# An expert stage that fetches its token rows by number inside its loop, with biases added by VectorE

## The chip, the cores and the metric

One Trainium2 chip, one of its cores. The time is that of one execution of the whole program on the device, in microseconds (us). The engines of a core are TensorE (PE), VectorE (DVE), ScalarE (ACT), GpSimd (POOL) and SyncE (SP); each runs its own list of instructions, and they wait for each other by semaphores. SP here only issues transfers; POOL issues those whose rows are chosen by a table of numbers in SBUF (indirect transfers).

## What is computed

A decoder layer on x of shape (8, 256, 256), so 2048 tokens of width D = 256: a gated linear branch, cross attention, self attention, and at its end a mixture of 8 experts, which is what the change is about:

```python
gp = softmax(xt @ w_group + b_group)          # 4 groups of 2 experts
g_idx, g_prob = argmax(gp), max(gp)
ep_sel = softmax(elog)[g_idx];  e_idx_local, e_prob = argmax(ep_sel), max(ep_sel)
flat_e = g_idx * 2 + e_idx_local              # one expert of 8 for each token
combine = one_hot(flat_e, E) * (g_prob * e_prob)
h = relu(einsum('td,edf->etf', xt, w1) + b1)  # 256 -> 512
y = einsum('etf,efd->etd', h, w2) + b2        # 512 -> 256
out = einsum('te,etd->td', combine, y)
x = layernorm(x + out)                        # of norm(x) with gain and bias
```

## The kernel before

`build` runs three stages with a barrier between them. `gate_stage` (in the profile 0 to 86 us) computes the weights of the linear branch from x @ qkv in a loop over pairs of batch rows; SP loads the next x of the pair as soon as TensorE has transposed the one before. Beside it GpSimd fills the DRAM table `xs_d` with zeros and a dummy token number (`blank`, L290 to L293, 5.9 MB). `attention_stage` (86 to 770 us) does both attentions, and writes for each batch row two results to DRAM: `x5_d` (the experts' input) and `x4_d` (the value to be added at the end). `w1`, the experts' first weights, is loaded at its start; it also makes an fp32r copy of a small table `chunk` (L1276).

`moe_stage` (770 us to the end) has two parts. The first sorts the tokens by expert: VectorE works out each token's expert, gate and rank (L1670 to L1742) with two small matrix products for the counts (L1586, L1587), and a row number `slot` in a table of 23 tiles of 128 rows (`TILES = NT + E - 1`, each tile of one expert, padded). SP loads all 2048 rows of `x5_d` and `x4_d` into `xr` (L1525, L1527); GpSimd writes them with 16 indirect transfers (L1558) to their places in `xs_d`, gate and token number among them as columns `GATE` and `TOKEN`. Then the second part runs over the 23 tiles. For tile c:

- SP loads the tile's 128 rows of `xs_d` into one of six buffers `xs` (L1536), once `u` of the tile six before is made.
- TensorE transposes it (L1599), multiplies with `w1` of the tile's expert (L1607), transposes the hidden rows (L1624) and multiplies with `w2` (L1616). The expert's number is read into a register from `texp_i` (`expert`, L1515) twice for each tile. Ahead of each of the two products a short fp32r product (L1605, L1614) puts the expert's bias into PSUM: `sel`, a 0/1 matrix, picks it from `bs`, which holds high and low parts of the biases.
- ScalarE moves the transposes from PSUM (L1642, L1652) and does the ReLU (L1647).
- VectorE: `first_b` to `first_e` (L1763 to L1777) scale by the gate, add the row itself and take mean and variance; `second_a` to `second_d` (L1784 to L1797) and `shift` (L1801) do the last normalisation. The parts of tile c and of tile c-1 are interleaved, so that hardly an instruction stands right behind the one it depends on.
- GpSimd takes two inverse roots for each tile (L1565, L1569) and writes the tile's output rows to their tokens (L1575, indirect).

TensorE's list is skewed by hand: the transposes of tile c+2, then the first product of tile c+1, then the second product of tile c-1, then the transposes of the hidden rows of tile c. `done(engine, semaphore, c)` is a wait for tile c.

Of the kernel before, what the change touches and what calls it, by code (L numbers as in the profile page):

```python
# [23 lines left out]
P = 128  # L24
# [15 lines left out]
ROW = 2 * D + 2  # L40
# [11 lines left out]
def build(nc, I, out):  # L52
# [8 lines left out]
    x4_d = scratch("x4_d", (B, P, T * D))  # L61
    x5_d = scratch("x5_d", (B, P, T * D))
    xs_d = scratch("xs_d", (TILES * P, ROW))

    outer = ExitStack()
    with outer:
# [18 lines left out]
        w1 = sbo("w1", [P, E, C, F])  # L85
        dense = outer.enter_context(ExitStack())

        def sbd(name, shape, dt=F32):
# [8 lines left out]
                 "bfeat": sbd("bfeat", [2 * C, 3, P]), "chunk": sbd("chunk", [2 * C, C * S]),  # L97
# [9 lines left out]
        def next_stage():  # L107
# [5 lines left out]
        gate_stage(nc, I, sem, ident, nhalf, stat, xsum, chan, wtok, dw, ahead, pT, pD, pS, vT_d, xs_d)  # L113
        next_stage()
        attention_stage(nc, I, sem, ident, nhalf, chan, wtok, logit, dw, w1, ahead, pT, pD, pW,
                        vT_d, x4_d, x5_d)
        next_stage()
        dense.close()
        moe_stage(nc, I, sem, ident, nhalf, logit, w1, bank, x4_d, x5_d, xs_d, out)
# [45 lines left out]
def gate_stage(nc, I, sem, ident, nhalf, stat, xsum, chan, wtok, dw, ahead, pT, pD, pS, vT_d, xs_d):  # L165
    with ExitStack() as ctx:
# [15 lines left out]
        blank = sb("blank", [P, ROW])  # L182
# [19 lines left out]
        def sems(names):  # L202
            return (sem("g_" + n) for n in names.split())

        w_in, small_in, w_hi, w_lo, mask0, masks, zero_ok, zero_out = sems(
            "w_in small_in w_hi w_lo mask0 masks zero_ok zero_out")
        dw_in, ahead_in = sems("dw_in ahead_in")
# [17 lines left out]
        def _(sp):  # L225
# [30 lines left out]
            sp.dma_start(ahead["chunk"][:, :], I["chunk"]).then_inc(ahead_in, 16)  # L256
# [3 lines left out]
            sp.wait_ge(ahead_in, 16 * 11)  # L260
# [5 lines left out]
        def _(pool):  # L266
# [19 lines left out]
            for m in (selb, selq):  # L286
# [3 lines left out]
            pool.memset(blank[:, 0:2 * D + 1], 0.0).then_inc(zero_ok, 1)  # L290
            pool.memset(blank[:, 2 * D + 1:ROW].bitcast(I32), B * S).then_inc(zero_ok, 1)
            pool.wait_ge(zero_ok, 2)
# [5 lines left out]
            pool.wait_ge(zero_out, 16)  # L298
# [124 lines left out]
        def _(dve):  # L423
# [128 lines left out]
            step(dve.tensor_copy(wtok[:, :, :].rearrange("p t b -> p (t b)"), pS[1][:, 0:T * B]))  # L552

# [66 lines left out]
def attention_stage(nc, I, sem, ident, nhalf, chan, wtok, logit, dw, w1, ahead, pT, pD, pW,  # L620
                    vT_d, x4_d, x5_d):
    with ExitStack() as ctx:
# [290 lines left out]
        def _(pe):  # L913
# [65 lines left out]
            def attention(i, l, a, beside):  # L979
                if i == 0 and a == 0 and l == 0:  # L980
                    pe.wait_ge(bias_ok, 5)
# [463 lines left out]
def moe_stage(nc, I, sem, ident, nhalf, logit, w1, bank, x4_d, x5_d, xs_d, out):  # L1445
    with ExitStack() as ctx:
# [97 lines left out]
        def _(pool):  # L1544
# [17 lines left out]
            for c in range(TILES + 4):  # L1562
# [8 lines left out]
                if there(c - 3):  # L1571
                    if c == 3:
                        pool.wait_ge(ids_in, 16)
# [313 lines left out]
```

## Time and profile before

| | us |
|---|---|
| median of 3 runs | 956.08 |
| lowest and highest | 943.71, 959.67 |
| the profiled execution | 957.81 |
| its span, from the first to the last instruction | 955.9 |
| mean granted TensorE clock in it (share of full) | 0.832 |

| stage | us in the profiled execution |
|---|---|
| gate stage | 0 to 86 |
| attention stage | 86 to 770 |
| expert stage, sorting | 770 to 815.2 |
| expert stage, 23 tiles | 815.2 to 955.9 |

Rows of the profile read: start, duration, engine, line, operation, output <- input, and in square brackets how long the engine had been idle before, and who ended that. A busy time of TensorE is modelled at its end, so the distance from start to start tells more than the duration. The biggest of these times, the attention stage, is touched by the change only at its edges.

### The profile page before, as it was taken

To read this page: it belongs to the slowest core of one execution; us is meant where nothing else is said; L and a number is where in the kernel's file an instruction comes from. 1 tells how busy PE (TensorE), PEld (TensorE's weight loads), DVE (VectorE), ACT (ScalarE), POOL (GpSimd) and SP (SyncE) were. 2 spreads that over 40 slices of the span, in tenths; PEclk is the share of its full clock that TensorE was granted. 3 is DMA by queue.
4 is the path that set the end of the run, shared out by engine and by line. 5 is a ranking of instruction groups with operands and counts; after the bars stand their busy time and mean duration, and the time that the engine had idled before them with its cause. 6 is when DMAs were issued, how large, how long until landed. Compare 5 with 4: busy or idle time off the path is not lost. (4 is left out here: it accounts for less than half of the span.)

```text
span 955.9 us, 11735 instructions
## 1 busy us (share of the span) xinstructions
PE 722.9 (76%) x4012; PEld 453.6 (47%) x4012; DVE 469.8 (49%) x1248; ACT 261.5 (27%) x397; POOL 182.4 (19%) x211
## 2 busy tenths in 40 slices
PE   4852487879887797878878888878896810899993
PEld 3741354545544454545545455544554410456562
DVE  1885165564653626455354745637456252044443
ACT  1101032323324221342404224232240300233432
POOL 1003410112201111220101122011110016034445
PEclk9985779988898867988779797987987655799997
DMA  9582612223112130311123031220303069222210
GB/s 281 147 278 70 195 35 67 50 64 78 46 34 68 46 80 32 78 46 34 51 62 84 30 78 46 57 56 2 78 2 89 3 219 328 67 61 69 77 59 14
DMA packets 66015, 77.88 MB, mean 81 GB/s; under 512 B 10758, under 2 KB 53459, under 8 KB 65832
## 3 DMA queue, kind: packets, MB, share of 16 engines
q1 hardware_dynamic: 60792, 62.56, 24.0%
q0 software_dynamic: 3872, 12.37, 4.1%
q10 hardware_dynamic: 1296, 2.23, 0.7%
q8 instruction: 33, 0.54, 0.2%
q14 instruction: 22, 0.18, 0.1%
HBM read 32.76 MB, written 19.57 MB: 55 GB/s over the span
## 5 line engine op out<-in xcount | busy, mean ns | idle before, releaser
L1337 DVE TENSOR_REDUCE a_nmax<-wide 128x4 f32<-128x1024 f32 x128 | 153.2, 1217 | 72.8 <-PE wide L975 72.3
L1187 ACT ACTIVATE a_E<-wide 128x1024 f32<-128x1024 f32 x128 | 123.5, 1013 | 50.6 <-PE wide L975 50.5
L857 POOL TENSOR_TENSOR a_rstd<-a_var,nhalf 128x2 f32<-128x2 f32 x40 | 27.9, 698 | 546.6 <-DVE a_var L1302 546.6
L133 PE MATMUL bank<-a_th,dw 128*128 128x256 f32 x320 | 108.0, 484 | 6.4 <-DVE a_x L1312 5.0
L975 PE MATMUL wide<-a_Q,a_K 50*128 50x256 f32 x512 | 73.3, 377 | 33.2 <-DMA a_Q<-a_mrow 18.6
L964 PE MATMUL bank<-a_E,a_va 128*32 128x256 f32 x1024 | 91.5, 490 | 0.0
L133 PE MATMUL bank<-dw,a_th 128*128 128x256 f32 x320 | 88.9, 412 | 0.0
L133 PEld LDWEIGHTS bank<-a_th,dw 128*128 128x128 f32 x320 | 70.5, 237 | 33.2 <-issue 14.3
L975 PE MATMUL wide<-a_K,a_Q 48*128 48x256 f32 x512 | 70.9, 363 | 20.3 <-DMA a_Q<-a_stage 13.0
L1166 ACT ACTIVATE a_th<-bank 128x512 f32<-128x512 f32 x48 | 28.6, 597 | 201.6 <-PE bank L922 201.6
L975 PEld LDWEIGHTS wide<-a_Q,a_K 50*128 50x128 f32 x512 | 46.0, 225 | 74.6 <-ACT a_E L1187 33.9
L133 PEld LDWEIGHTS bank<-dw,a_th 128*128 128x128 f32 x320 | 62.5, 205 | 28.6 <-ACT a_th L1166 10.0
L975 PEld LDWEIGHTS wide<-a_K,a_Q 48*128 48x128 f32 x512 | 43.9, 212 | 62.8 <-issue 37.5
L1763 DVE SCALAR_TENSOR_TENSOR m_z<-wide,m_xs 128x256 f32<-128x256 f32 x23 | 11.1, 484 | 96.9 <-PE wide L133 96.9
L1288 DVE TENSOR_TENSOR a_stage<-bank,a_stage 128x256 fp32r<-128x256 f32 x64 | 24.1, 419 | 65.2 <-ACT a_stage L1174 65.2
L1359 DVE COPY a_cu<-bank 128x256 f32<-128x256 f32 x64 | 25.7, 419 | 49.3 <-PE bank L964 49.3
L133 PE MATMUL bank<-w,m_xT 128*128 x92 | 49.2, 660 | 0.0
L964 PEld LDWEIGHTS bank<-a_E,a_va 128*32 128x32 f32 x1024 | 31.9, 129 | 32.3 <-issue 22.2
L133 PE MATMUL wide<-m_w,m_hT 128*128 x184 | 45.9, 392 | 0.9 <-ACT m_hT L1652 0.9
L1174 ACT ACTIVATE a_stage<-bank 128x512 fp32r<-128x512 f32 x32 | 19.1, 597 | 74.4 <-PE bank L133 67.2
L133 PEld LDWEIGHTS wide<-m_w,m_hT 128*128 128x128 f32 x184 | 33.1, 189 | 7.5 <-issue 1.3
L1198 ACT ACTIVATE a_mrow<-bank 8x256 fp32r<-8x256 f32 x32 | 12.0, 374 | 89.3 <-PE bank L1026 88.7
(256 smaller groups left out, 985.0 us busy)
## 6 DMA issues: line engine op xcount, KB each, us to landing
a_K<-a_stage SPq DMA_DIRECT2D x96, 128.0 KB, 3.2
a_Q<-a_stage SPq DMA_DIRECT2D x96, 128.0 KB, 3.5
xs_d<-g_blank POOLq DMA_DIRECT2D x1, 5911.0 KB, 28.2
m_xs<-xs_d SPq DMA_DIRECT2D x23, 257.0 KB, 2.7
w<-in_w_dram SPq DMA_DIRECT2D x1, 4096.0 KB
x_d<-a_x SPq DMA_DIRECT2D x16, 256.0 KB, 2.7
m_xr<-x_d SPq DMA_DIRECT2D x16, 256.0 KB, 5.5
m_w<-in_w_dram SPq DMA_DIRECT2D x1, 4096.0 KB, 24.8
```

Source lines behind the costliest of these rows:

```text
L133: last = pe.matmul(out, left[c], right[c], start=(start and c == 0), stop=(stop and c == n - 1))
L857: pool.tensor_tensor(rstd[l][:, :], var[l][:, :], nhalf[:, 0:T], ALU.pow).then_inc(rs_ok[l].s, 1)
L964: last = pe.matmul(bank[32 * h:32 * h + 32, 0:S], va[l][:, kt, HC * (h // 2) + 2 * g + h % 2, :], Ex[g % 2][:, kt, h, :], start=(kt == 0), ...
L975: last = pe.matmul(pW[r % 2][:, c * 512 + e * S:c * 512 + (e + 1) * S], left[l][part_, s, tok(t)], right[l][part_, s, :], start=True, stop ...
L1166: act.activation(halves(dst[l]), pT[l][:, :], ACT.Copy).then_inc(done[l].s, 1)
L1174: act.activation(stage[l][:, x_, :, 0, :], bank[l][:, :].rearrange("p (c s) -> p c s", c=C), ACT.Copy).then_inc(done[l].s, 1)
L1187: act.activation(Ex[g % 2][:, kt, :, :], pW[r % 2][:, :].rearrange("p (h s) -> p h s", h=4), ACT.Exp, scale=HD ** -0.5).then_inc(ex.s, 1)
L1198: act.activation(mrow[:, h, 0, :], pT[l][0:HC, h * S:(h + 1) * S], ACT.Copy).then_inc(mx_hi[l].s, 1)
L1288: last = dve.tensor_tensor(stage[l][:, x_, c, 1, :], bank[l][:, c * S:(c + 1) * S], stage[l][:, x_, c, 0, :].bitcast(F32), SU)
L1337: dve.tensor_reduce(nmax[l][:, t, :].rearrange("p (h c q e) -> p h q c e", h=HALVES, c=C, q=2)[:, jj // 2, jj % 2, :, :], pW[r % 2][:, :]. ...
L1359: dve.tensor_copy(cu[:, g, :], (pT, pD)[g % 2][l][:, 0:S]).then_inc(cu_ok[l].s, 1)
L1763: dve.scalar_tensor_tensor(z[c % 2][:, :], pY[c % 2][:, 0:D], xs[c % XB][:, GATE:GATE + 1], xs[c % XB][:, 0:D], MM, AD).then_inc(z_ok, 1)
```

## The change

- `xs_d`, `x4_d`, `x5_d` and `xr` are gone, with the fill in the gate stage. The attention stage writes both results side by side into one table `xc_d` of 2048 rows of 512 columns, in token order (pieces of 1 KB instead of 2 KB).
- The numbers of the tokens of each tile are made by 16 matrix products: `place` (a 0/1 matrix for each block of 128 tokens: which row in its tile) times `want` (for each token: its tile, times 1, its number or its gate). The sum is `ids` (number), `gates` and, by the empty places, `oids` (output number, out of bounds where the place is empty).
- GpSimd fetches each tile's rows from `xc_d` with an indirect transfer `gather(c)`: four before the loop, and one in each turn, four tiles ahead. SP's loads are gone.
- The bias products, `sel`, `bs` and what made them are gone. `b2` is loaded spread over all partitions (1 MB) in the attention stage behind `w1`, `b1` (2 MB) at the start of the expert stage ahead of `w2`. VectorE adds them when it moves the products out of PSUM: `inner(c)` for 512 columns, `first_a(c)` for 256. VectorE reads the expert's number into a register for each. ScalarE's ReLU now sits in the move of the hidden transposes, and its move L1647 is gone.
- VectorE's list in the loop is rewritten: `inner` of the next tile, the second half of one tile, the first half of the next, with pairs that depend on each other closer together.
- TensorE waits for `w2` only before the first product that uses it. The copy of `chunk` moves to the end of the gate stage.

```diff
-            pool.dma_start(xs_d.rearrange("(p n) d -> p n d", p=P),
-                           blank[:, :].unsqueeze(1).to_broadcast([P, TILES, ROW])).then_inc(zero_out, 16)
...
+            dve.wait_ge(chunk_in, 16)
+            dve.tensor_copy(ahead["chunk_r"][:, :], chunk[:, :])
...
+            sp.dma_start(b2[:, :, :], I["b2"].partition_broadcast(P)).then_inc(w1_in, 16)
...
-            for b in range(B):
-                sp.dma_start(xr[:, b * T:(b + 1) * T, 0:D], x5_d[b].rearrange("p (t d) -> p t d", t=T)).then_inc(x5_in, 16)
...
+            sp.dma_start(b1[:, :, :], I["b1"].partition_broadcast(P)).then_inc(b_in, 16)
             sp.dma_start(w2[:, :, :, :], I["w2"].rearrange("e (c p) f -> p e c f", p=P)).then_inc(w_in, 16)
...
-            for n in range(NT):
-                pool.indirect_dma_start(out=xs_d, out_offset=bass.IndirectOffsetOnAxis(ap=slot[:, n:n + 1], axis=0),
-                                        in_=xr[:, n, :], in_offset=None).then_inc(xs_w, 16)
+            def gather(c):
+                done(pool, u_ok, c - XB)
+                pool.indirect_dma_start(out=xs[c % XB][:, :], out_offset=None, in_=xc_d,
+                                        in_offset=bass.IndirectOffsetOnAxis(ap=ids[:, c:c + 1], axis=0)
+                                        ).then_inc(xs_in[c % XB], 16)
+            pool.wait_ge(id_ok, 1)
+            for c in range(AHEAD):
+                gather(c)
             for c in range(TILES + 4):
+                if there(c + AHEAD):
+                    gather(c + AHEAD)
...
+            for n in range(NT):
+                if n % 4 == 0:
+                    pe.wait_ge(place_ok, n // 4 + 1)
+                last = pe.matmul(bank[0][:, 0:3 * TILES], place[:, n, :], want[:, n, :, :].rearrange("p k c -> p (k c)"),
+                                 start=(n == 0), stop=(n == NT - 1))
...
-                    pe.matmul(pH[l][:, :], sel[:, c + 1, :], bs[:, 0:F], start=True, stop=False)
-                    pe.matmul(pY[l][:, 0:D], sel[:, c - 1, :], bs[:, F:], start=True, stop=False)
...
-                    act.activation(hb[l][:, :], pH[l][:, :], ACT.Relu).then_inc(hb_ok, 1)
-                    act.activation(halves(hT[l]), pHT[l][:, :], ACT.Copy).then_inc(hT_ok, 1)
+                    act.activation(halves(hT[l]), pHT[l][:, :], ACT.Relu).then_inc(hT_ok, 1)
...
+            step(dve.tensor_scalar(r16[1][:, :], r16[0][:, :], 1.0 / P, None, MM))
+            step(dve.tensor_tensor(over, r16[1][:, :].unsqueeze(2).to_broadcast([P, NT, TILES]),
+                                   cst[:, NT:].unsqueeze(1).to_broadcast([P, NT, TILES]), ALU.is_ge))
+            step(dve.tensor_reduce(r16[2][:, :], over, AX.X, AD))
+            step(dve.scalar_tensor_tensor(r16[4][:, :], r16[2][:, :], -float(P), r16[0][:, :], MM, AD))
+            dve.tensor_tensor(want[:, :, 2, :], over, past[:, :, 1:], SU).then_inc(want_ok, 1)
+            for n in range(0, NT, 4):
+                dve.tensor_tensor(place[:, n:n + 4, :], line[:, :].unsqueeze(1).to_broadcast([P, 4, P]),
+                                  r16[4][:, n:n + 4].unsqueeze(2).to_broadcast([P, 4, P]), ALU.is_equal).then_inc(place_ok, 1)
...
+            dve.tensor_copy(ids[:, :], bank[0][:, 0:TILES]).then_inc(id_ok, 1)
...
+            def inner(c):
+                e = expert(dve, c)
+                done(dve, h_mm, c)
+                done(dve, h_tr, c - 2)
+                dve.tensor_tensor(hb[c % 2][:, :], pH[c % 2][:, :], b1[:, bass.ds(e, 1), :].rearrange("p o f -> p (o f)"), AD
+                                  ).then_inc(hb_ok, 1)
...
+            for c in range(-1, TILES + 3):
+                if there(c + 1):
+                    inner(c + 1)
+                if there(c - 2):
+                    second_a(c - 2)
+                    second_b(c - 2)
+                if there(c - 3):
+                    shift(c - 3)
+                if there(c - 1):
+                    first_a(c - 1)
+                if there(c - 2):
+                    second_c(c - 2)
+                if there(c - 1):
+                    first_b(c - 1)
+                if there(c - 2):
+                    second_d(c - 2)
+                if there(c - 1):
+                    first_c(c - 1)
+                    first_d(c - 1)
+                    first_e(c - 1)
```

## Rows read from the trace of the kernel before

**Rows 1.** By stretch: length; busy PE, PEld, DVE, ACT, POOL; PEclk; DMA share; GB/s.
```profile
815.20:829.00 13.80, 13.61 (x28) 5.69 (x28) 0.00 (x0) 3.00 (x7) 0.00 (x0) 0.61 0.35 78
860.00:890.00 30.00, 30.00 (x118) 18.77 (x118) 12.84 (x54) 11.64 (x23) 13.03 (x18) 1.00 0.23 72
```

**Rows 2.** Timeline: TensorE in one turn of the tile loop.
```profile
852.45 0.38 PE L1599 MATMUL bank<-ident,m_xs 128*128 128x128 f32 x2
852.76 0.49 PE L1605 MATMUL bank<-m_bs,m_sel 16*128 16x512 f32 x1
853.18 1.98 PE L133 MATMUL bank<-w,m_xT 128*128 x4
855.09 0.38 PE L1614 MATMUL wide<-m_bs,m_sel 16*128 16x256 f32 x1
855.40 1.99 PE L133 MATMUL wide<-m_w,m_hT 128*128 x8
857.23 0.60 PE L1624 MATMUL wide<-ident,m_hb 128*128 128x128 f32 x4
```

**Rows 3.** Timeline: VectorE, the first tile's product read and one turn later on.
```profile
831.40 0.48 DVE L1763 SCALAR_TENSOR_TENSOR m_z<-wide,m_xs 128x256 f32<-128x256 f32 x1 [36.80 <-PE wide L133]
...
857.43 0.48 DVE L1763 SCALAR_TENSOR_TENSOR m_z<-wide,m_xs 128x256 f32<-128x256 f32 x1 [2.90 <-PE wide L133]
```

**Rows 4.** Timeline: from the rank of each token to the first tile.
```profile
788.65 0.29 DVE L1741 TENSOR_TENSOR m_rank<-m_rank,m_oh 128x128 f32<-128x128 f32 x1
788.97 0.29 DVE L1742 TENSOR_REDUCE m_r<-m_rank 128x16 f32<-128x128 f32 x1
...
790.35 1.07 POOL L1558 DMA_INDIRECT xs_d<-m_xr,m_slot  x1 [14.16 <-DVE m_slot L1743]
...
809.47 0.96 POOL L1558 DMA_INDIRECT xs_d<-m_xr,m_slot  x1 [0.31 <-issue]
...
815.21 1.29 PE L1599 MATMUL bank<-ident,m_xs 128*128 128x128 f32 x4 [32.39 <-DMA m_xs<-xs_d]
```

**Rows 5.** Timeline: gate stage, TensorE's and VectorE's wait in its first turn.
```profile
22.45 0.66 PE L315 MATMUL wide<-ident,g_x 128*128 128x128 f32 x4 [3.85 <-DMA g_x<-in_x_dram]
...
30.10 0.69 DVE L435 TENSOR_REDUCE xsum<-wide 128x512 f32 x1 [1.00 <-ACT g_xh L393]
```

**Rows 6.** Transfers: issue, count, KB each, median us from issue to landing.
```profile
g_x<-in_x_dram SPq DMA_DIRECT2D x8, 256.0 KB, 4.1
...
xs_d<-g_blank POOLq DMA_DIRECT2D x1, 5911.0 KB, 28.2
...
out_dram<-m_o,m_ids POOLq DMA_INDIRECT x23, 2.5
```

**Rows 7.** Groups of instructions: busy us and mean ns, VectorE on 184 and 512 columns.
```profile
L1745 DVE TENSOR_TENSOR m_cmp_t<-m_cst,m_ntile 128x184 f32<-128x184 f32 x1 | 0.3, 343 | 0.0
...
L1420 DVE TENSOR_TENSOR a_va<-bank,rows 128x512 f32<-128x512 f32 x8 | 5.5, 692 | 2.9 <-PE bank L133 2.9
```

**Rows 8.** Timeline: the first of the two small products of the sorting.
```profile
781.62 0.77 PE L1586 MATMUL wide<-m_oh,m_low 128*128 128x128 f32 x2 [12.68 <-DVE m_oh L1705]
782.18 0.63 PE L1587 MATMUL wide<-m_oh,m_ones 128*128 128x128 f32 x2
```

**Rows 9.** Line L1515, TensorE's register loads: ns min/median/max, first and last start.
```profile
L1515 PEldq TENSOR_LOAD <-m_texp_i x46: 295/301/526, 815.8 to 937.2; - x46
L1515 PEldq FUSED_REGOPS  x46: 151/151/171, 816.4 to 937.6; - x46
```

**Rows 10.** Timeline: GpSimd in one turn of the tile loop.
```profile
854.17 0.73 POOL L1565 TENSOR_TENSOR m_rstd<-m_var,nhalf 128x1 f32<-128x1 f32 x1 [2.77 <-DVE m_var L1776]
...
855.60 1.03 POOL L1575 DMA_INDIRECT out_dram<-m_o,m_ids  x1 [0.19 <-issue]
```

**Rows 11.** Busy time of two output transfers' issue, columns as in Rows 1.
```profile
942.12:943.15 1.03, 0.00 (x0) 0.00 (x0) 1.03 (x4) 0.00 (x0) 1.03 (x1) 1.00 0.00 0
855.60:856.63 1.03, 1.03 (x6) 0.90 (x6) 0.00 (x0) 0.20 (x1) 1.03 (x1) 1.00 0.00 0
```

More of the change, by code:

```diff
@@ L159, in __call__, with gate_stage @@
         self.eng.wait_ge(self.sem, self.i * self.per + self.base + self.n)
-def gate_stage(nc, I, sem, ident, nhalf, stat, xsum, chan, wtok, dw, ahead, pT, pD, pS, vT_d, xs_d):
+def gate_stage(nc, I, sem, ident, nhalf, stat, xsum, chan, wtok, dw, ahead, pT, pD, pS, vT_d):
     with ExitStack() as ctx:
@@ L255, in _ @@
             sp.dma_start(ahead["bfeat"][:, :, :], I["bfeat"]).then_inc(ahead_in, 16)
-            sp.dma_start(ahead["chunk"][:, :], I["chunk"]).then_inc(ahead_in, 16)
+            sp.dma_start(chunk[:, :], I["chunk"]).then_inc(chunk_in, 16)
             sp.dma_start(ahead["part"][:, :], I["part"]).then_inc(ahead_in, 16)
@@ L627, in both @@
             return [sb(f"{name}{l}", shape, dt) for l in range(2)]
-        cin, x, pos, rows, brow, bfeat, chunk, part, wr = (
-            ahead[n] for n in "cin x pos rows brow bfeat chunk part wr".split())
-        chunk_r = sb("chunk_r", [2 * C, C * S], F32R)
+        cin, x, pos, rows, brow, bfeat, chunk_r, part, wr = (
+            ahead[n] for n in "cin x pos rows brow bfeat chunk_r part wr".split())
         bsplit = sb("bsplit", [2 * C, 3, P], F32R)
@@ L1441, with moe_stage @@
 XB, UB = 6, 4
-GATE, TOKEN = 2 * D, 2 * D + 1
-def moe_stage(nc, I, sem, ident, nhalf, logit, w1, bank, x4_d, x5_d, xs_d, out):
+AHEAD = 4
+def moe_stage(nc, I, sem, ident, nhalf, logit, w1, b2, bank, xc_d, out):
     with ExitStack() as ctx:
@@ L1453, in moe_stage @@
         w2 = sb("w2", [P, E, FC, D])
-        bias = sb("bias", [E, F + D])
-        bs, bl = sb("bs", [2 * E, F + D], F32R), sb("bl", [E, F + D], F32R)
-        which = some(3, "which", [2 * E, 1])
-        at16 = sb("at16", [2 * E, 2 * E])
-        sel = sb("sel", [2 * E, TILES, P], F32R)
-        xr = sb("xr", [P, NT, ROW])
+        b1 = sb("b1", [P, E, F])
+        past = sb("past", [P, NT, TILES + 1])
+        want = sb("want", [P, NT, 3, TILES])
+        place = sb("place", [P, NT, P])
+        line = sb("line", [P, P])
+        gate = sb("gate", [P, NT])
+        gates = sb("gates", [P, TILES])
+        free = sb("free", [P, TILES])
         gain = sb("gain", [P, D])
@@ L1629, in _ @@
             act.dma_start(gain[:, :], I["rows"][R_FG2].partition_broadcast(P)).then_inc(c_in, 16)
-            act.wait_ge(b_in, 32)
-            act.activation(bs[0:E, :], bias[:, :], ACT.Copy).then_inc(b_hi, 1)
             act.wait_ge(g_in, 1)
@@ L1802, in shift @@
                                          ).then_inc(mr_ok, 1)
-            for c in range(TILES + 2):
-                now, old, older = there(c), there(c - 1), there(c - 2)
-                if now:
-                    first_b(c)
-                if old:
-                    second_a(c - 1)
-                if now:
-                    first_c(c)
-                if old:
-                    second_b(c - 1)
-                if now:
-                    first_d(c)
-                if old:
-                    second_c(c - 1)
-                if older:
-                    shift(c - 2)
-                if now:
-                    first_e(c)
-                if old:
-                    second_d(c - 1)
+            for c in range(-1, TILES + 3):
[18 more added lines that the diff above has]
+                    first_e(c - 1)
 def layouts(inputs):
```

146 lines of the change are left out of this document (62 added, 84 removed).

## The prediction

> **What bounds the kernel now.** I read four views in this order: the stages by stretch, the timeline of the expert stage, the groups of instructions, and the first turns of the gate stage. In the 30 us between 860 and 890 us TensorE is busy for all 30, at a granted clock of 1.00 (2.4 GHz), while VectorE is busy for 12.84 and GpSimd for 13.03 [rows 1]. So the tile loop is bound by TensorE. One turn is, from start to start: input transposes 0.31, bias product 0.42, first product 1.91, bias product 0.31, second product 1.83, hidden transposes to the turn's end 0.44 [rows 2], together 5.22. VectorE's starts say the same: (857.43 - 831.40) / 5 = 5.21 [rows 3].
>
> Ahead of the loop stands a serial stretch. The tokens' ranks are done at 788.97 + 0.29 = 789.26; 16 scatters leave GpSimd from 790.35 to 809.47, one each 1.27; the last must land and be read back before the transposes at 815.21 [rows 4]. That is 25.95 us in which TensorE does nothing. In the gate stage TensorE waits 3.85 us for an x tile and VectorE 1.00 in the turn behind [rows 5], while the fill of `xs_d` takes 28.2 us to land; the median x load takes 4.1 [rows 6].
>
> **The change part by part.** The sum is made against the profiled execution, 957.81 us, which lies 1.7 above the median of 956.08.
>
> *Gate stage, -4.85 and +0.7.* Without the fill the third x load should take the usual 4.1 us. It is issued when TensorE has transposed the first tile, which is before the first products, so it is there well before TensorE's products end at 22.45 - 3.85 = 18.6. The 3.85 goes. The turn behind it waited 1.00 more on VectorE [rows 5]; from there on VectorE paces the stage, and keeps what it got. I take 4.85 (bounds 0, if the load is late for another reason, and 4.85). The copy of `chunk`, 512 columns, now stands at the end of VectorE's list: 0.69 by another 512-column operation [rows 7]. At its old place its cover was TensorE's and ScalarE's work, so nothing comes back there.
>
> *Attention stage, +0.2.* 1 MB more behind the 4 MB of `w1` is queued on SP ahead of the first key rows. In the stretches that I looked at, the DMA engines stand still for some microseconds before the query rows that the first scores wait for, so this is hidden; without that cover it costs some 3 us. Rows of 1 KB instead of 2 may let the last store land a little later: 0 to 0.5.
>
> *Sorting to first tile, -11.6.* New, behind 789.26, on VectorE: a 16-column scale 0.2; compare, reduce and difference on 16 x 23 = 368 columns. 184 columns take 0.34 and 512 take 0.69 [rows 7], so 0.54 each, and 0.03 from the end of one to the start of one that needs it [rows 4]: 3 x 0.57, with a small one of 0.22: 2.1 so far. Two more of 368 columns 0.9, the first `place` 0.69: 793.0. Then 16 products of 69 moving columns. The product of 128 columns takes 0.56 from start to start [rows 8]; if all of it goes with the columns one is 0.30, if nothing 0.56. I take 0.40, 6.4 together (bounds 4.8 and 9.0), for both matrices must be loaded, whatever moves. VectorE makes the four `place` groups in 4 x 0.69, faster than they are used. 799.4. Copy of the numbers 0.3, GpSimd's start 0.8 (its first scatter came that much behind `slot` [rows 4]), and one gather from issue to landing: not in the trace; the output writes need 2.5 [rows 6], the last scatter and its read-back together 815.21 - 809.47 = 5.7. It is nearest to the former, but of double size: 3.1. First tile there at 803.6 instead of 815.21. `b1` and `w2`, 6 MB, have 30 us for it and replace 4 MB of `xr` and 4 MB of `w2`; VectorE's wait for `b1` is covered by that.
>
> *First turns, -1.6.* Up to the first VectorE read of a second product at 831.40 [rows 3] three long and one short bias products fall away: 3 x 0.42 + 0.31 [rows 2]. The mean granted clock is 0.61 here [rows 1], so mostly the lower level of 1.2 GHz; there they were longer, but the same clock may then last into later work.
>
> *The loop, -17.5.* TensorE: without the two bias products 5.22 - 0.42 - 0.31 = 4.49 at most. The rest can shrink too. Four hidden transposes take 0.11 each; at that rate (128 columns in 0.11) the fp32 products, 1024 columns in two passes, would take 1.76 and two input transposes 0.22 [rows 2]: 1.76 + 1.76 + 0.44 + 0.22 = 4.18. What is above it in the rows stands where fp32 and fp32r products take turns, which ends. So 4.2 to 4.5.
>
> VectorE: busy now 12.84 / 30 x 5.22 = 2.23 each tile [rows 1]. `inner` adds 0.69 [rows 7], `first_a` about 0.42 (half the columns, with the fixed part), and the new order puts some five instructions right behind the one that they need; each loses the overlap of neighbours and 0.03: about 0.1, with a little more 0.4. That is 3.7. Then two register loads, each 0.30 + 0.15 on TensorE's sequencer [rows 9]. VectorE has none in this trace. Each comes behind an instruction of 0.4 to 0.5 us that is already under way, which covers most: 0 to 0.9 for both, I take 0.3. VectorE 4.0, at worst 4.6. `inner` stands ahead of `second_a`, `second_b` and `shift`, so whoever waits for these (GpSimd's second root, ScalarE's output move) gets them later, but they have a turn of slack.
>
> The Trainium skill (DMA: Bandwidth & Descriptors, section Latency and other measured facts) gives a floor of about 600 ns for such a load; here 301 ns is the median. By the page the turn of VectorE would be up to 4.9 and 0.6 x 19 = 11 us of the gain gone.
>
> GpSimd: from the first root to the end of the output's issue 855.60 + 1.03 - 854.17 = 2.46 [rows 10]. A gather adds 0.96 and 0.30 [rows 4]: 3.7. So TensorE stays the slowest, by little. With three engines this close some waits will appear: 4.3. There are 19 full turns (the last three have no first product): 19 x (5.22 - 4.3) = 17.5.
>
> *Tail, +0.5.* The last tile has `first_a` on its way out.
>
> Sum: -4.85 + 0.7 + 0.2 - 11.6 - 1.6 - 17.5 + 0.5 = -34.15; 957.8 - 34.2 = 923.6. I predict 923. Its own range: turn 4.2 to 4.5, products 4.8 to 9.0: 915 to 933.
>
> **The rivals.**
>
> *A. VectorE becomes the bound.* If its sequencer can't load a register while an instruction runs, the loads are bare: 3.7 + 0.9 = 4.6, and with waits for the semaphores up to 4.9. 4.75 gives 8.6 us less gain: 932. For it: the new order is tight, and VectorE's register loads are unseen. Against it: TensorE's loads cost it nothing, its busy time has no gap [rows 1, 9].
>
> *B. GpSimd becomes the bound.* Its issues and roots might have to wait while VectorE works: at most one VectorE instruction (0.48 [rows 3]) for each of four GpSimd instructions, 3.7 + 1.9 = 5.6: loop gain gone, 949. Against it: an output's issue took 1.03 with VectorE busy throughout and 1.03 with VectorE idle [rows 11]. Here stands a rule that speaks against the change: the Trainium skill (SBUF — State Buffer, section SBUF: two separate sides) says that a VectorE instruction with two SBUF inputs and GpSimd exclude each other from a shared port; `first_b` now has two. The trace agrees in part only: the first root takes 0.73, but the issues do not stretch [rows 10, 11].
>
> *C. Slower.* One mechanism could do it: VectorE's register load costs far more than TensorE's, with nothing hidden. All gains but the loop's are 34.15 - 17.5 = 16.65; they are used up when a turn takes 5.22 + 16.65 / 19 = 6.1, that is at 1.2 us for each load; over 2% slower (975) needs 1.6 to 1.7. At 1.7: a turn of 7.1, 923.6 + 2.8 x 19 = 977. TensorE's slowest load was 0.53 [rows 9].
>
> *D. The fill was not what held the x load.* Then 4.85 stays: 928.
>
> *E. Faster still.* The 16 products bring the full clock forward and the loop runs at 4.2 with the first turns at full clock as well (stretch at 0.61 of full, 13.8 us [rows 1]: up to 5 us less): 916.
>
> **How the numbers follow.** Forecast 0.52, A 0.23, B 0.07, C 0.03, D 0.05, E 0.10. The range for 8 in 10 takes in forecast, A, D and E and their ends, 909 to 938; left out are B, C and some unknown. About 2% is what this kernel's measurement can tell from no change (the runs shown lie 1.7% apart), so faster means below 937. Forecast, A, D and E are faster, 0.90, less what a mis-sized sum may take: 0.87. B and part of that: 0.10 within 2%. C: 0.03.
>
> **What would show it.** Gate: the 3.85 wait at L315 is gone. Sorting: first transposes 14 to 15 us behind the rank's reduction, 16 products in about 6.4. Loop: starts of the second product 4.3 apart, no idle time of TensorE; if VectorE is without a gap and TensorE waits for `inner` or `first_a`, it is A; if `second_a` waits for the first root and GpSimd has no gap, B. Wrong it would be by a gather that lands far later than 3.1 us, or by an attention stage that runs otherwise although nothing in it was changed.

## The result: slower, with the gain of every part but one

| | before | after |
|---|---|---|
| median | 955.43 (4 runs) | 971.69 (4 runs) |
| lowest and highest | 943.71, 959.67 | 970.90, 977.05 |
| profiled execution | 957.81 | 971.45 |
| its span | 955.9 | 969.7 |
| mean granted TensorE clock | 0.832 | 0.830 |

The ratio of the medians is 1.017; the ratio recorded with its 95% interval is 1.0224 (1.0123 to 1.0325): slower, and whether by more than 2% is left open. The forecast was 923, range 909 to 938.

Where the 13.8 us between the two spans come from, each part read from the two timelines:

| part | before | after | difference |
|---|---|---|---|
| gate stage, to the last copy of `wtok` | 85.40 | 79.66 | -5.7 |
| from there to the expert stage's first instruction | 685.4 | 682.7 | -2.7 |
| from there to the ranks | 18.4 | 14.8 | -3.6 |
| ranks to the first tile's transposes | 25.95 | 15.17 | -10.8 |
| first tile's transposes to the end | 140.7 | 177.4 | +36.7 |

Ahead of the tile loop the execution is 22.9 us shorter, where 15.6 were forecast. The last part got 36.7 longer, where it was forecast to get 18.6 shorter (first turns, loop and tail). So the whole miss, and more, lies in the last part.

The same span grows and shrinks from run to run in the attention stage, which no kernel here touches within: in the profiles of the changed kernel and of its variants without the fill the expert stage begins anywhere from 754.97 to 773.45. Some executions lie more than 1.5% above the fastest of their kernel (three of four of `e11_all`, two of four of `e3_ahead6`, two of ten of `e6_busygap`, one of four of `e2_ahead5`), and the medians given below include them. So all kernels below are compared by the stretch from the first tile's transposes to the end of the span, read from one profiled execution each. How much this stretch varies between executions of one kernel was not measured, so differences of about 1 us are read only where the rows show where they lie.

The loop after. TensorE's rows, two undisturbed turns and then one with a wait (start, duration, engine, line, operation; in brackets the idle time before and who ended it):

```profile
801.42 0.60 PE L1609 MATMUL wide<-ident,m_hb 128*128 128x128 f32 x4
801.85 0.38 PE L1584 MATMUL bank<-ident,m_xs 128*128 128x128 f32 x2
802.07 1.88 PE L132 MATMUL bank<-w,m_xT 128*128 x4
803.79 1.89 PE L132 MATMUL wide<-m_w,m_hT 128*128 x8
805.52 0.60 PE L1609 MATMUL wide<-ident,m_hb 128*128 128x128 f32 x4
...
809.62 0.60 PE L1609 MATMUL wide<-ident,m_hb 128*128 128x128 f32 x4
812.38 0.44 PE L1584 MATMUL bank<-ident,m_xs 128*128 128x128 f32 x2 [2.16 <-DMA m_xs<-xc_d,m_ids]
```

A turn that nothing holds takes 805.52 - 801.42 = 4.10, against 5.22 before [rows 2]: the expected gain is there. But from the sixth tile on every second turn waits for the gathered rows, and the wait grows. The view of waits, 830 to 960 us (us in total, times, longest):

```profile
PEld bank L1584 <- DMA m_xs<-xc_d,m_ids: 30.3, 7, 5.2
PE bank L1584 <- DMA m_xs<-xc_d,m_ids: 28.6, 7, 5.0
```

The same by stretch: TensorE is busy for 109 of 146 us, at a granted clock of 0.86, where before it was busy for all of its 30 at 1.00 [rows 1]:

```profile
803.79:950.00 146.21, 109.14 (x383) 69.40 (x381) 77.03 (x247) 29.12 (x60) 62.33 (x76) 0.86 0.15 46
```

Neither VectorE (77 of 146) nor GpSimd (62) is anywhere near full. What holds the loop is not an engine's work but a chain that goes round through TensorE, VectorE, GpSimd and the transfer. One round of it, two turns long, from the timeline of all engines:

```profile
869.25 0.69 PE L1584 MATMUL bank<-ident,m_xs 128*128 128x128 f32 x2 [4.05 <-DMA m_xs<-xc_d,m_ids]
...
870.10 3.78 PE L132 MATMUL bank<-w,m_xT 128*128 x4 [0.17 <-issue]
...
873.67 2.70 PE L132 MATMUL wide<-m_w,m_hT 128*128 x8
...
874.63 0.48 DVE L1787 SCALAR_TENSOR_TENSOR m_u<-m_z,m_rstd,m_xs 128x256 f32<-128x256 f32 x1
...
876.52 0.42 DVE L1760 TENSOR_TENSOR m_y<-wide,b 128x256 f32<-128x256 f32 x1 [0.89 <-PE wide L132]
...
878.18 0.15 DVE L1779 TENSOR_SCALAR m_var<-m_mv 128x1 f32<-128x1 f32 x1
878.25 0.47 DVE L1780 SCALAR_TENSOR_TENSOR m_z<-m_z,m_mv,m_gain 128x256 f32<-128x256 f32 x1
878.42 0.74 POOL L1544 TENSOR_TENSOR m_rstd<-m_var,nhalf 128x1 f32<-128x1 f32 x1 [7.27 <-DVE m_var L1779]
...
879.14 0.54 POOL L1548 TENSOR_TENSOR m_rstd<-m_var,nhalf 128x1 f32<-128x1 f32 x1
...
879.87 1.06 POOL L1554 DMA_INDIRECT out_dram<-m_o,m_oids  x1 [0.19 <-issue]
...
881.24 0.99 POOL L1530 DMA_INDIRECT m_xs<-xc_d,m_ids  x1 [0.30 <-issue]
...
884.60 0.44 PE L1584 MATMUL bank<-ident,m_xs 128*128 128x128 f32 x2 [3.68 <-DMA m_xs<-xc_d,m_ids]
```

Read it as one sum: transposes to first product 0.85, first product 3.57, second product to VectorE's read 2.85, first half of the normalisation 1.90, first root 0.72, second root 0.73, output issue 1.37, gather to the next transposes 3.36: 15.35 from wait to wait. The gather is four tiles ahead by its number. By its place it is not: it stands in GpSimd's list behind the first root of a tile, that root needs the tile's second product, and TensorE's list is skewed, so that when this product ends, the transposes of the tile that the gather fetches are due two turns later. Two turns must hold the chain. When nothing waits they last 8.2.

And the wait costs twice. The first product behind it takes 3.78, twice the 1.88 of an undisturbed one, and the granted clock from 869.25 to 873.60 us is 0.50: TensorE comes out of the wait at the lower level, 1.2 GHz. The second takes 2.70 instead of 1.89; from 876.60 to 880.50 us the granted clock is 1.00 again, 2.4 GHz.

### The profile page after: what moved, and what is told of

Read it like the earlier page. It is cut to its first block and busy times, and to the rows that moved or that the text cites. A ratio compares the mean times of both kernels' runs of the same rounds, so it can differ in the third digit from the quotient of the medians.

```text
span 969.7 us, 11952 instructions
## 1 busy us (share of the span) xinstructions
PE 718.0 (74%) x4000; PEld 456.4 (47%) x4000; DVE 500.9 (52%) x1304; ACT 247.3 (25%) x373; POOL 187.3 (19%) x214
## 5 line engine op out<-in xcount | busy, mean ns | idle before, releaser
L132 PE MATMUL bank<-a_th,dw 128*128 128x256 f32 x320 | 105.8, 476 | 6.3 <-DVE a_x L1304 5.0
L957 PE MATMUL bank<-a_E,a_va 128*32 128x256 f32 x1024 | 89.3, 479 | 0.3 <-DVE a_cu L1351 0.3
L132 PEld LDWEIGHTS bank<-a_th,dw 128*128 128x128 f32 x320 | 69.6, 234 | 33.0 <-issue 14.5
L132 PE MATMUL bank<-w,m_xT 128*128 x92 | 60.2, 789 | 3.0 <-issue 1.8
L1753 DVE TENSOR_TENSOR m_hb<-bank,m_b 128x512 f32<-128x512 f32 x23 | 15.9, 692 | 69.3 <-PE bank L132 67.9
L132 PEld LDWEIGHTS wide<-m_w,m_hT 128*128 128x128 f32 x184 | 38.8, 212 | 21.3 <-issue 16.7
L1584 PE MATMUL bank<-ident,m_xs 128*128 128x128 f32 x46 | 11.1, 330 | 38.7 <-DMA m_xs<-xc_d,m_ids 38.7
```

The lines of the kernel that those rows point to most:

```text
L132: last = pe.matmul(out, left[c], right[c], start=(start and c == 0), stop=(stop and c == n - 1))
L957: last = pe.matmul(bank[32 * h:32 * h + 32, 0:S], va[l][:, kt, HC * (h // 2) + 2 * g + h % 2, :], Ex[g % 2][:, kt, h, :], start=(kt == 0), ...
```

## The experiments

The theory (Q in the first expectations) is that the gather's place in GpSimd's list makes it late. Its rivals are gathers that are slow by themselves, a VectorE or GpSimd full of work, and the low clock as the cause and not the effect.

### Five and six tiles ahead

```diff
-XB, UB = 6, 4
-AHEAD = 4
+XB, UB = 7, 4
+AHEAD = 5
```

> Edit: gathers five tiles ahead in place of four, seven tile buffers in place of six. Theory Q (queue lead): the gather of tile t+5 stands on GpSimd behind the first root of tile t, so only two turns must hold first product, second product, VectorE's first half, both roots, the output's issue, the gather's issue and its landing, 12.6 us without the low clock, 15.3 with it. One tile more gives three turns for 12.6, which is 4.2 each: TensorE's waits for the fetched rows (28.6 us in the loop) nearly vanish, its clock stays high, a turn is 4.1 to 4.3, the time 915 to 925. Rival S (VectorE or GpSimd is full): the turn is theirs, buffers change nothing, 960 to 972. Rival T (the fetch itself is too slow for a turn): waits stay, 950 or more.

Measured: 921.84 (916.48 to 932.45), ratio 0.9608, 95% interval 0.9526 to 0.9689. The stretch from the first transposes to the end is 917.6 - 792.02 = 125.6. TensorE, 820 to 880 us, is busy for 56.9 of 60 at full clock:

```profile
820.00:880.00 60.00, 56.94 (x238) 38.29 (x237) 49.31 (x160) 19.06 (x39) 45.33 (x54) 1.00 0.27 82
```

Two constants turn a kernel some 2% slower than before into one 4% faster. They had to change together, since a gather reuses the buffer of an earlier tile, but a free buffer is not what the gathers of the changed kernel wait for. The buffer of the one issued at 881.24 above had been free since 875.11, when VectorE had read it for the last time (the row at 874.63). Six ahead, with eight buffers:

> Edit: gathers six tiles ahead, eight tile buffers. Theory Q: four turns for 12.6 us, no wait at all, the turn is TensorE's own 4.1; within 3 us of the run with five ahead (912 to 922). Rival S: 960 to 972. Rival T: what is too slow each turn stays too slow with more buffers, 950 or more.

Measured: 928.68 (912.08 to 935.53), ratio 0.9718 (0.9648 to 0.9787), stretch 910.3 - 784.90 = 125.4. The stretch is the same as with five ahead. The reason is that VectorE sets the pace of both: from its first to its last read of a second product, 22 turns, it is 97.7 us with five ahead and 97.5 with six, 4.4 a turn.

### The gather moved up in GpSimd's list

```diff
             for c in range(TILES + 4):
-                if there(c + AHEAD):
-                    gather(c + AHEAD)
                 if there(c):
                     done(pool, var1_ok, c)
                     pool.tensor_tensor(rstd1[c % 2][:, :], ...)
+                if there(c + AHEAD + 1):
+                    gather(c + AHEAD + 1)
```

> Edit: same number of buffers and same tiles ahead, only the order on GpSimd: each gather is issued right behind the first root, ahead of the second root and the output's transfer. Theory Q: the round trip loses the second root and the output's issue, 0.54 + 0.19 + 1.06, about 1.8 us in two turns, nine or ten times: 952 to 957, waits of TensorE for the rows 2 us instead of 4 each, still every second turn. Rival T or S: the queue's order does not matter, 970.

Measured: 947.45 (944.56 to 950.35), ratio 0.989 (0.9813 to 0.9967), stretch 948.6 - 797.88 = 150.7. Five gathers now stand ahead of the loop instead of four (not shown), and the one behind a tile's first root is for the same tile as before, five on. It now follows that root at once:

```profile
853.95 0.73 POOL L1542 TENSOR_TENSOR m_rstd<-m_var,nhalf 128x1 f32<-128x1 f32 x1 [1.71 <-DVE m_var L1779]
854.87 1.00 POOL L1530 DMA_INDIRECT m_xs<-xc_d,m_ids  x1 [0.19 <-issue]
855.90 0.58 POOL L1548 TENSOR_TENSOR m_rstd<-m_var,nhalf 128x1 f32<-128x1 f32 x1
```

From the first root to the gather's issue it is 0.92 instead of 2.82. That is 1.9 less in the chain, and the loop is 26.7 us shorter, some 1.4 a turn, more than the chain alone accounts for. The waits (14.2 us in all, 16 times, 2.0 at most) now hardly bring the clock down: it is 0.97 between 820 and 880 us, against 0.86. The time is some 5 us below the range expected.

### Rows loaded by SyncE

```diff
+            for c in range(TILES):
+                done(sp, u_ok, c - XB)
+                r = c % NT
+                sp.dma_start(xs[c % XB][:, :], xc_d[r * P:(r + 1) * P, :]).then_inc(xs_in[c % XB], 16)
```

The gathers are out of GpSimd's list. This leaves out which rows belong to a tile: it takes them in the table's order.

> Edit: no gathers; SyncE loads 128 rows one after the other for each tile, in table order, with the same waits for buffers (which rows belong to the tile is left out, so the output is not the layer's). VectorE's added biases and register loads all stay. Theory Q: SyncE's list has nothing in front, a load is issued when its buffer is free; turn 4.1, 910 to 920. Rival S, VectorE full by its biases: the turn stays, 960 to 972.

Measured: 922.30 (920.50 to 924.09), ratio 0.9627 (0.9557 to 0.9697), stretch 918.7 - 796.93 = 121.8. Against before's 140.7 that is -18.9, beside the forecast's -18.6 (-1.6 -17.5 +0.5), with everything in the loop as the change has it except who fetches the rows and how. From 804.79 to 882.72 TensorE makes 18 turns in 4.33 each; 4.3 was forecast. That the two sums agree so closely is in part luck. Up to VectorE's first read of a second product 4.4 us are won and not 1.6, in the 22 turns from there to its last read 13.3 and not 17.5 (97.2 against 110.5), and behind it 1.2 are won where 0.5 was to be lost.

### Three ahead

```diff
-AHEAD = 4
+AHEAD = 3
```

> The changed kernel with the rows fetched three tiles ahead instead of four. Theory (the gather stands in GpSimd's list behind the first root of an earlier tile, so a chain of about 15.3 us with the low clock has to fit in the turns between): now it has to fit in one turn instead of two, and a turn takes 15 to 16.5 us instead of 7.2: about 19 turns x 8.5 = +160, 1115 to 1150. Rival (the gathers are slow by themselves, 23 of them at a fixed rate on GpSimd or the DMA engines, whatever the lead): 970 to 990.

Measured: 1128.12 for one execution, stretch 322.9. With a lead of one turn every turn is a round of the chain:

```profile
895.53 0.69 PE L1584 MATMUL bank<-ident,m_xs 128*128 128x128 f32 x2 [7.75 <-DMA m_xs<-xc_d,m_ids]
910.36 0.69 PE L1584 MATMUL bank<-ident,m_xs 128*128 128x128 f32 x2 [8.01 <-DMA m_xs<-xc_d,m_ids]
924.62 0.69 PE L1584 MATMUL bank<-ident,m_xs 128*128 128x128 f32 x2 [8.04 <-DMA m_xs<-xc_d,m_ids]
```

Three, four and five ahead give some 15.0, 7.1 to 7.6 and 4.4 to 4.6 us a turn. A turn lasts the chain divided by the turns that it has, until TensorE's or VectorE's own turn is longer: this is the theory. Gathers at a rate of their own would have shown the same time in all three, and a gather takes the same from issue to landing in all three (median 3.4 to 3.6).

### TensorE kept busy through the wait

```diff
+                    done(pe, xT_ok, c)
+                    if c + 2 >= 5 and (c + 2) % 2 == 1:
+                        for _ in range(32):
+                            pe.transpose(pX[l][:, 0:P], ident[:, :], ident[:, :])
                     pe.wait_ge(xs_in[(c + 2) % XB], 16 * ((c + 2) // XB + 1))
-                    done(pe, xT_ok, c)
```

Work is added here that nobody reads.

> The changed kernel with 32 transposes of 128 columns that nobody reads added on TensorE ahead of the wait for the rows of every odd tile from 5 on, so that TensorE works through most of the wait. Theory (the wait costs twice: by itself, and by the granted clock that falls in it, with the next two products at 3.78 and 2.70 us instead of 1.88 and 1.89): with the clock kept, the two products take 1.9 each, a round trip of two turns takes some 12.6 instead of 15.3, 8 round trips, about -20 us: 950 (946 to 956), waits still there. Rival (the low granted clock comes from something else, or the extra work only delays): 970 or more.

Measured: 964.61 (953.82 to 970.89, 10 runs), ratio 1.0088 (1.0040 to 1.0135), stretch 958.8 - 794.37 = 164.4, 13.0 less than in the changed kernel. One of these stretches, GpSimd's gather with it:

```profile
863.03 0.99 POOL L1530 DMA_INDIRECT m_xs<-xc_d,m_ids  x1 [0.30 <-issue]
...
863.94 3.66 PE L1584 MATMUL bank<-ident 128*128 128x128 f32 x32
...
867.43 0.38 PE L1587 MATMUL bank<-ident,m_xs 128*128 128x128 f32 x2
...
867.65 1.88 PE L132 MATMUL bank<-w,m_xT 128*128 x4
```

More work, less time: with the granted clock at 1.00 throughout (820 to 880 us) the product takes 1.88 instead of 3.78. The direction is as expected, the size is 13 of 20. The rest is the added work itself: at 3.36 from issue to use the rows are there at 866.4, but TensorE is through with the 32 transposes only at 867.4, some 1 us late in each of the rounds, which take 13.4 (six of them from 840.79 to 921.36) instead of 15.3. Without the added work and at full clock the chain would be 12.3: 8.90 from the transposes at 867.43 to the next gather's issue at 876.33, and 3.36. That is still 6.1 a turn, more than the 5.22 of before. So the gather's place alone makes the loop slower than before, and the clock adds to it.

### The fill back in its place

```diff
+            pool.memset(blank[:, :], 0.0).then_inc(zero_ok, 1)
+            pool.wait_ge(zero_ok, 1)
+            pool.dma_start(fill_d.rearrange("(p n) d -> p n d", p=P),
+                           blank[:, :].unsqueeze(1).to_broadcast([P, TILES, ROW + 2])).then_inc(zero_out, 16)
```

A transfer is added here into a table that nobody reads.

> The changed kernel with one thing added: the old fill of 5.9 MB with zeros is back at its old place in the gate stage, into a tensor that nothing reads. If the fill is what held the third x load, TensorE waits some 3.9 us for it again at L306's transposes and the last copy of the gate stage on VectorE moves from 79.7 us back to about 85.4 (+5.7). Rival: the load was held by something else of the old kernel, and the last copy stays within 1 us of 79.7.

Measured: 987.94 for one execution. The wait is back, and the last copy of `wtok` stands at 87.34 instead of 79.66, +7.7:

```profile
24.11 1.11 PE L314 MATMUL wide<-ident,g_x 128*128 128x128 f32 x4 [5.07 <-DMA g_x<-in_x_dram]
```

So the fill held the x load. The wait and the delay are both larger than in the kernel before (5.07 against 3.85, 87.34 against 85.40), and why is not shown. The rest of the 16.5 us by which the execution is longer than the profiled one of the changed kernel lies in the attention stage (691.4 against 682.7), which the edit does not touch and whose length changes by itself; one execution can't tell more.

### What binds once the rows are there in time

With five ahead TensorE's turns are 4.10 up to some 820 us and 4.2 to 4.9 behind. VectorE in the kernel whose rows SyncE loads, one turn of it:

```profile
873.50 0.69 DVE L1754 TENSOR_TENSOR m_hb<-bank,m_b 128x512 f32<-128x512 f32 x1 [0.28 <-issue]
...
874.96 0.14 DVE L1805 SCALAR_TENSOR_TENSOR m_mr<-m_mv,m_rstd 128x1 f32<-128x1 f32 x1
875.43 0.42 DVE L1761 TENSOR_TENSOR m_y<-wide,b 128x256 f32<-128x256 f32 x1 [0.34 <-issue]
...
877.91 0.69 DVE L1754 TENSOR_TENSOR m_hb<-bank,m_b 128x512 f32<-128x512 f32 x1 [0.27 <-issue]
```

Its turn is 877.91 - 873.50 = 4.41 and its only idle times are the 0.28 and 0.34 ahead of the two additions, where its register loads stand. TensorE, at 4.10, gets ahead of it by 0.3 each turn and is held up when its lead is used up. Three kernels try this.

```diff
+OB = 3
-                    if k >= 2:
-                        act.wait_ge(out_w[k % 2], 16 * (k // 2))
+                    if k >= OB:
+                        act.wait_ge(out_w[k % OB], 16 * (k // OB))
```

> Rows fetched five tiles ahead with seven buffers, and three output buffers instead of two. ScalarE's output move no longer waits for an output's landing (21 us in all in the kernel with five ahead alone). If TensorE alone sets the turn there (4.10), that is worth nothing: 0.961 of the kernel before, within 0.5% of the kernel with five ahead. Rival: the waits of ScalarE reach TensorE through its moves of the transposed tiles: up to 0.3 us a turn in the later turns, 3 to 6 us less, 916.

Measured: 924.73 (918.12 to 931.50), ratio 0.9692 (0.9637 to 0.9748), stretch 925.4 - 799.02 = 126.4. The third output buffer is worth nothing in the turns, as expected, though TensorE's 4.10 is not the reason: VectorE's 4.41 is. At the very end it is worth 1.0 us: from VectorE's last scaling by the gate to the end of the last output's issue it is 8.3 us instead of 9.3, since ScalarE no longer waits for an output to land ahead of each of its last moves.

```diff
             def inner(c):
-                e = expert(dve, c)
+                e = held[c] = expert(dve, c)
             def first_a(c):
-                e = expert(dve, c)
+                e = held.pop(c)
```

> The kernel with rows fetched five ahead, in which VectorE loads each tile's expert number into a register once, ahead of the first addition, and keeps it for the second one two turns later, instead of loading it twice. Theory: once the rows are there in time, VectorE's list is the longest, and its two register loads are bare (0.28 and 0.34 us of a turn of 4.41 in the kernel that loads its rows by plain transfers). One load less, and VectorE takes 4.07 to 4.13, so the later turns go from 4.4 to 4.6 back to 4.10 to 4.2: from the first tile's transposes to the end 125.6 - 12 x 0.35 = some 121.5 us, a ratio to the kernel before lower by about 0.004. Rival: the later turns are long for another reason (the output's landing, GpSimd's list), and this stretch stays at 125 to 126 us.

> The same with three output buffers. Theory: VectorE's list alone, so no difference to two buffers: 121.5 us from the first tile to the end. Rival: with VectorE shorter, ScalarE's wait for an output's landing is the next bound (its wait was 21 us in all with two buffers): two buffers 123 to 125 and three 121 us.

Measured: 925.25 (916.67 to 928.79), ratio 0.9664 (0.9587 to 0.9741), stretch 125.4; and with three output buffers 916.61 (912.66 to 920.36), ratio 0.9589 (0.9525 to 0.9653), stretch 124.2. Both expectations missed, 121.5 was expected. The first came out as its rival has it (125 to 126, the later turns long for another reason). The 1.2 between the two is mostly the 1.0 that the third output buffer gives at the end. VectorE did get shorter, and the second load's gap is gone, here with two output buffers:

```profile
859.28 0.14 DVE L1806 SCALAR_TENSOR_TENSOR m_mr<-m_mv,m_rstd 128x1 f32<-128x1 f32 x1
859.44 0.42 DVE L1762 TENSOR_TENSOR m_y<-wide,b 128x256 f32<-128x256 f32 x1
```

What it gave was taken back by the old wait, since a shorter turn makes a lead of three turns shorter too (3 x 4.10 = 12.3, just the chain at full clock): the 22 turns last 97.4 and 97.3, as without the change. From the timeline of the kernel with three output buffers:

```profile
854.32 0.44 PE L1585 MATMUL bank<-ident,m_xs 128*128 128x128 f32 x2 [1.69 <-DMA m_xs<-xc_d,m_ids]
860.67 0.38 PE L1585 MATMUL bank<-ident,m_xs 128*128 128x128 f32 x2
```

A wait of 1.69, and the turn behind it takes 6.35 instead of 4.10. Hence the last kernel, with three output buffers, one register load and six ahead. Against the kernel just shown only the lead and the number of tile buffers differ:

> Rows fetched six ahead with eight buffers, three output buffers, one register load a tile on VectorE. Theory: with five ahead and one register load the turns were 4.10 where nothing disturbed them, and what was left between 121.5 and 124.2 us were waits for rows (1.7 us at one place) with short falls of the granted clock behind them; so five ahead is only just enough at 4.10 a turn. With six ahead no wait is left: 121 to 122 us from the first tile's transposes to the end, every turn 4.10 to 4.2. Rival: the long turns have another cause (transfers landing later when more of them are under way), and it stays at 124 or more.

Three turns of it, and 60 us by stretch:

```profile
849.79 0.38 PE L1585 MATMUL bank<-ident,m_xs 128*128 128x128 f32 x2
853.89 0.38 PE L1585 MATMUL bank<-ident,m_xs 128*128 128x128 f32 x2
857.99 0.38 PE L1585 MATMUL bank<-ident,m_xs 128*128 128x128 f32 x2
```

```profile
820.00:880.00 60.00, 60.00 (x265) 42.19 (x264) 54.41 (x178) 20.32 (x45) 48.92 (x57) 1.00 0.29 86
```

Measured: 918.03 (901.60 to 926.15), stretch 915.4 - 799.30 = 116.1, the shortest of all, and shorter than the 121 to 122 expected. From 812.88 us on every turn is 4.10, and TensorE is busy for 60 of 60 us. The lead alone is worth 124.2 - 116.1 = 8.1 here, and was worth nothing (125.6 and 125.4) while VectorE's turn was 4.41. Against 954.70 for the kernel before beside it the medians stand at 0.962; no interval is given, for the reason above. By the stretch it is 24.6 us below the kernel before and 61.3 below the changed one.

| kernel | fetch | first transposes to the end |
|---|---|---|
| before | SyncE, six buffers | 140.7 |
| after | four ahead | 177.4 |
| `e8_ahead3` | three ahead | 322.9 |
| `e1_order` | four ahead, behind the first root | 150.7 |
| `e6_busygap` | four ahead, TensorE kept busy | 164.4 |
| `e2_ahead5`, `e7_outs3` | five ahead | 125.6, 126.4 |
| `e3_ahead6` | six ahead | 125.4 |
| `e4_direct` | SyncE, no gathers | 121.8 |
| `e9_onereg`, `e10_both` | five ahead, one register load | 125.4, 124.2 |
| `e11_all` | six ahead, one load, three outputs | 116.1 |

## Why the prediction was wrong, step by step

**The step that failed** is "A gather adds 0.96 and 0.30 [rows 4]: 3.7. So TensorE stays the slowest, by little." It priced the gather as work on GpSimd and asked only whether the engine would be full. It never asked when a gather is issued, and what it stands behind. Nor did any rival: B is GpSimd full of work, C a slow register load. The change is described as "four tiles ahead", and the prediction took that number for the lead. What the runs showed in its place is a chain of 15.3 us that has two turns, so 7.1 to 7.6 us a turn where 4.3 was forecast. Before, the loads were in SyncE's list, which held nothing else, so a load left as soon as a buffer came free. The change moved them into a list where each stands behind a root that waits for VectorE.

**It could have been worked out** from the rows at hand. Input transposes 0.31, first product 1.91, second 1.83 [rows 2], from VectorE's read of a second product to the first root 1.96 (854.17 less one turn before 857.43 [rows 2, 3, 10]; the added bias makes it somewhat more, the new order less), first root to the end of the output's issue 2.46 [rows 10], a gather from issue to landing 3.1 as forecast: 11.6, with the gaps some 12. In two turns that is 6 each, above the 5.22 of before. The loop would then be 19 x 0.8 = 15 us longer instead of 17.5 shorter, and the sum 956, before anything for the clock. The measured chain is 12.3 at full clock and 15.3 as it ran.

**The gate stage**: -4.85 and +0.7 forecast, -5.7 and +0.4 measured. The mechanism was right (`e5_fill`), rival D is out, but the gain lies above the 4.85 that was given as the most. The copy of `chunk` took 0.41 and not 0.69:

```profile
79.66 0.17 DVE L543 COPY wtok<-wide 128x16 f32<-128x16 f32 x1 [0.47 <-PE wide L369]
79.86 0.41 DVE L545 CAST chunk_r<-g_chunk 4x512 fp32r<-4x512 f32 x1
```

**The attention stage**: +0.2 forecast. It lasts 2.7 less in this execution, but since it changes by more than that from one execution to the next, nothing can be told of the step.

**Up to the ranks**: forecast at nothing, measured -3.6, a gain that was overlooked. Before, ScalarE's copy of the biases `bs` stood ahead of the first Exp and waited for their load, and VectorE with it; then GpSimd's subtraction for the low parts ran beside VectorE. Before:

```profile
774.23 0.24 ACT L1633 ACTIVATE m_gx<-m_gl 128x64 f32<-128x64 f32 x1
...
774.40 1.79 POOL L1552 TENSOR_TENSOR m_bl<-m_bias,m_bs 8x768 fp32r<-8x768 f32 x1 [2.90 <-ACT m_bs L1631]
774.50 0.22 DVE L1676 TENSOR_REDUCE m_r<-m_gx 128x16 f32<-128x64 f32 x1 [2.67 <-ACT m_gx L1633]
...
775.04 1.24 DVE L1678 TENSOR_TENSOR m_gp<-m_gx,m_r 128x64 f32<-128x64 f32 x1
```

After:

```profile
763.81 0.23 DVE L1656 TENSOR_TENSOR m_gp<-m_gx,m_r 128x64 f32<-128x64 f32 x1
```

2.67 of wait and 1.24 - 0.23 = 1.0 of the same instruction make the 3.6.

**Ranks to the first tile**: 14.3 forecast, 15.17 measured. The products, 6.4 forecast, took from 781.06 to the copy of the numbers at 788.24, 7.2, a little above; the rest is as priced:

```profile
781.06 7.07 PE L1572 MATMUL bank<-m_want,m_place 128*128 128x69 f32 x32 [10.42 <-DVE m_place L1733]
...
788.24 0.18 DVE L1742 CAST m_ids<-bank 128x23 int32<-128x23 f32 x1 [4.45 <-PE bank L1572]
...
788.72 1.19 POOL L1530 DMA_INDIRECT m_xs<-xc_d,m_ids  x1 [25.69 <-DVE m_ids L1742]
...
792.33 0.66 PE L1584 MATMUL bank<-ident,m_xs 128*128 128x128 f32 x2 [4.20 <-DMA m_xs<-xc_d,m_ids]
```

The gather is there 3.6 behind its issue, 3.1 was forecast; over all 23 it is 3.2 to 4.7, median 3.5. That is not what "far later" meant as a warning at the prediction's end: the landing was as fast as forecast, the issue was late.

**First turns, loop and tail**: -1.6, -17.5 and +0.5 forecast. VectorE's first and last read of a second product, after:

```profile
805.83 0.42 DVE L1760 TENSOR_TENSOR m_y<-wide,b 128x256 f32<-128x256 f32 x1 [1.03 <-PE wide L132]
...
955.15 0.42 DVE L1760 TENSOR_TENSOR m_y<-wide,b 128x256 f32<-128x256 f32 x1 [0.34 <-issue]
```

Before, they stand at 831.40 [rows 3] and 941.92. From the first transposes to the first read it is 13.5 instead of 16.2, so -2.7; from the last read to the end 14.5 instead of 14.0, +0.6; the 22 turns between take 149.3 instead of 110.5, +38.8. So the failure is in the turns alone.

**The turn**: TensorE 4.10, just under the 4.18 given as the least. VectorE was put at 4.0, at worst 4.6, and takes 4.41: the two register loads are bare by 0.6 and not 0.3. So rival A's mechanism is real, at two thirds of its size, and hidden behind the fetch in the changed kernel. Taken together the forecast of 4.3 a turn was nearly right for a loop whose rows are there in time: in `e4_direct` TensorE's turns are 4.33 in the mean, those of VectorE, which sets the pace in the end, 4.42.

**The other rivals.** B is out: GpSimd is busy for 43% of the loop, and `first_b`, with its two SBUF inputs, takes 0.48 to 0.49, and the outputs' issues 1.0 to 1.2. C foresaw the sign, but not by this mechanism: a load costs 0.3, not 1.2. E did not come: the granted clock from 792.3 to 803.8 us is 0.66, with the 16 products ahead of it. The prediction's own range, 915 to 933, does not follow from the bounds that it names either: a turn of 4.2 to 4.5 and products of 4.8 to 9.0 give 920 to 930.

## What to carry to other kernels

How far ahead a transfer is issued is not the number in the code but the distance between the instruction that it stands behind in its engine's list and its use: follow that chain through all engines, once round, and divide it by the turns that it may last. Do this for every transfer that changes its queue, above all from a queue that does nothing else into one that also computes. And where the chain is longer than its turns, the wait comes at every round, grows by what the TensorE clock loses in it, and eats the gain of every shortened turn.

## What the runs showed of the hardware

- After a wait of 1.69 us (granted clock 1.00 in it, 0.59 in the 4.2 us behind it) TensorE's next turn took 6.35 instead of 4.10; after one of 4.05 the next two products took 3.78 and 2.70 instead of 1.88 and 1.89. Filling the wait with products that nobody reads kept the granted clock at 1.00 and made the loop 13 us shorter.
- With the fp32r products between them gone, the fp32 products take 0.1 to 0.2 us less from start to start: 1.72 and 1.73 (802.07, 803.79, 805.52), where it was 1.91 and 1.83 before. So TensorE's turn lost 1.12 us and not only the 0.73 of the two bias products. No run separates the types from the mere number of products.
- Ahead of an addition that needs a register load VectorE stands idle for 0.27 to 0.35 us, behind a short instruction (0.14) and also behind one of 0.47. With one load left out its gap is gone and the turn goes from 4.42 to 4.08.
- One VectorE instruction with two SBUF inputs, 64 columns, took 1.24 us while GpSimd's subtraction ran (it ended 0.09 behind it) and 0.23 without; the reduction at 774.50, with one input, took its usual 0.22 beside it. The Trainium skill (SBUF — State Buffer, section SBUF: two separate sides) says that such a pair excludes each other for a whole instruction; this row agrees. In the tile loop, where GpSimd works on one column, no VectorE instruction is stretched so. But GpSimd's first root, which starts 0.17 behind the start of such a VectorE instruction (878.25, 878.42), takes 0.74, and the second root, of the same size and with no such instruction beside it, 0.54. It is so in every turn, and before the change too; no run separates the two.
